# A decoder layer in float32: loaded operands of the Q, K and V products placed 64 bytes ahead of the streaming ones

## The reference

```
q = x Wq (16 heads of 64);  k = x Wk, v = x Wv (8 groups of 64)
x = norm(x + softmax(mask(q k^T / 8)) v Wout + b_out)          # causal self-attention
xn = norm(x) * ln_w + ln_b;  q = xn Wq' / 8 (8 heads of 64)
x = norm(x + cross(q, ctx Wkv', mask) Wout')                   # over 77 context rows, at most 5 allowed ones
x = norm(x + (silu(x Wg) * (x Wu)) Wd)                         # 768 hidden, integer weights / 127
```

## The kernel before, in words

| product (fills) | loaded | streaming | matmuls a batch |
|---|---|---|---|
| Q, K (nQ0, aQ1 to aQ3, nK0, aK1) | wq, wk | xTs | 72 of 256 columns |
| V (aV0, aV1) | xTs | wv | 12 of 512 columns |
| OUT (oOUT0, oOUT1) | Z | wo | 48 of 256 |
| XQ | xwq | NX | 24 of 256 |
| XV | ctxs (77 columns) | xwv | 6 of 512 |
| XOUT | H | xwo | 24 of 256 |
| FFN (gate and up) | wg, wu | NT | 72 of 256 |
| DOWN | H | wd | 36 of 256 |

## Time and profile before

### The profile page before, as it was taken

One profiled execution on the slowest core, in us unless ns is written; L12 is line 12 of the kernel. 1 busy time (PEld: TensorE's weight loads), 2 busy tenths in 40 slices (PEclk: granted clock), 3 DMA queues, 4 the chain that ended last, 5 costly groups with the idle time before them and its releaser, 6 DMA issues.

```text
span 2029.4 us, 50598 instructions
## 1 busy us (share of the span) xinstructions
PE 2000.8 (99%) x18176; PEld 1837.8 (91%) x18176; DVE 1545.9 (76%) x5708; ACT 1324.1 (65%) x3992; POOL 377.6 (19%) x624
## 2 busy tenths in 40 slices
PE   8999999999999999999999999999999999999987
PEld 7899999999999999999999999999999999999886
DVE  6877777777777777777777777777777777777764
ACT  8866666667666666666666666666666666666642
POOL 3112111211211111112121112112121211121121
PEclk9999999999999999999999999999999999999998
DMA  5100000000000000000000000000000000000000
GB/s 164 32 8 22 19 21 12 11 19 19 22 12 19 11 19 22 19 12 22 8 21 19 12 22 8 22 19 22 12 19 11 19 22 19 12 11 19 13 7 11
DMA packets 49606, 41.19 MB, mean 20 GB/s; under 512 B 19536, under 2 KB 47568, under 8 KB 49360
## 3 DMA queue, kind: packets, MB, share of 16 engines
q1 hardware_dynamic: 49360, 37.96, 6.4%
HBM read 29.56 MB, written 8.39 MB: 19 GB/s over the span
## 4 chain that ended last, share of the span: by engine, by line
PE 97%; DVE 1%; ACT 1%; issue 1%; SPq 0%; DMA 0%; POOL 0%; POOLq 0%; DVEq 0%; ACTq 0%
PE gen L442 20%; PE gen L443 19%; PE gen L444 19%; PE s_ps L582 9%; PE z_ps L624 7%; PE gen L530 3%; PE pt_ps L603 3%; PE gen L543 3%; PE gen L539 3%; PE pt_ps L604 3%; PE pt_ps L608 3%; PE z_ps L626 3%; PE gen L510 2%; PE gen L501 1%; PE gen L554 1%
## 5 line engine op out<-in xcount | busy, mean ns | idle before, releaser
L955 ACT ACTIVATE SM<-SM,least 128x128 f32<-128x128 f32 (+1 forms) x1024 | 452.4, 447 | 35.1 <-DVE least L1480 35.0
L885 ACT ACTIVATE PT<-pt_ps 128x512 f32<-128x512 f32 (+1 forms) x512 | 237.8, 486 | 237.6 <-PE pt_ps L604 235.4
L1480 DVE CUSTOM_DVE_ANT_0 SM<-s_ps,causal 128x128 f32<-128x128 f32 (+1 forms) x1024 | 314.6, 352 | 19.6 <-PE s_ps L582 14.7
L1493 DVE TENSOR_SCALAR SM<-SM,total 128x128 f32<-128x128 f32 (+1 forms) x1024 | 282.7, 339 | 9.1
L1859 POOL TENSOR_TENSOR H_lo<-gated,H_hi 128x256 fp32r<-128x256 f32 x192 | 143.2, 752 | 513.0 <-ACT H_hi L885 513.0
L582 PE MATMUL s_ps<-KT,QT 64*128 64x128 f32 (+1 forms) x2048 | 201.5, 335 | 1.4 <-ACT KT L885 0.7
L938 ACT ACTIVATE gated<-gen 128x256 f32<-128x256 f32 x192 | 73.8, 385 | 197.6 <-PE gen L444 197.5
L955 ACT ACTIVATION_READ_ACCUMULATOR SM<-SM,least 128x1 f32 x1024 | 197.0, 192 | 0.0
L1457 DVE SCALAR_TENSOR_TENSOR gated<-gated,gen 128x256 f32<-128x256 f32 x192 | 80.9, 421 | 115.8 <-ACT gated L938 115.4
L624 PE MATMUL z_ps<-PT,Vt 128*64 128x256 f32 x1024 | 168.1, 399 | 0.0
L582 PEld LDWEIGHTS s_ps<-KT,QT 64*128 64x128 f32 x2048 | 147.6, 187 | 21.8 <-issue 6.4
(11 more groups left out here) (185 smaller groups left out, 6504.7 us busy)
## 6 DMA issues: line engine op xcount, KB each, us to landing
xT_in<-in_xT SPq DMA_DIRECT2D x32, 256.0 KB, 2.9
x_in<-in_x SPq DMA_DIRECT2D x32, 256.0 KB, 2.8
out<-rows SPq DMA_DIRECT2D x32, 256.0 KB, 2.2
ctx_in<-in_ctxT SPq DMA_DIRECT2D x32, 77.0 KB, 2.8
mask_in<-in_maskT SPq DMA_DIRECT2D x32, 77.0 KB, 2.6
SX<-in_wq SPq DMA_DIRECT2D x1, 512.0 KB, 6.4
rows<-in_wv SPq DMA_DIRECT2D x1, 512.0 KB, 7.2
xwk<-in_xwkv SPq DMA_DIRECT2D x1, 512.0 KB, 7.9
```

The source lines that it names most:

```text
L885: return act.activation(o, i, ACT.Copy)
L955: ins = act.activation(part, part, ACT.Exp, scale=-1.0, bias=least[:, i % 4, n:n + 1], accum_out=total[:, i % 4, n:n + 1])
L1480: ins = dve.tensor_tensor_reduce(SM[:, i % 4, at:at + keys], s_ps[bank][:, col:col + keys], causal[:, S - keys:S], -SCALE, -3 * NEG, ALU.a ...
L1493: ins = dve.tensor_scalar(part, part, total[:, i % 4, n:n + 1], None, ALU.mult)
```

## The change

The order of allocation is altered and nothing else. Every tensor keeps its size, and every instruction its operands by name.

```diff
@@ -187,21 +187,21 @@
-        wq_s = halves("wq", [P, KD, HE])
-        wk_s = halves("wk", [P, KD, KE])
         xwq_s = halves("xwq", [P, KD, XE])
         wg_s = halves("wg", [P, KD, HID])
         wu_s = halves("wu", [P, KD, HID])
+        xT_s = halves("xTs", [P, KD, S])
+        least = sb("least", [P, 4, 4])
+        wv_s = halves("wv", [P, KD, KE])
         den = sb("den", [P, T, 2, XH])
-        wv_s = halves("wv", [P, KD, KE])
-        xwv_s = halves("xwv", [P, KD, XE])
-        least = sb("least", [P, 4, 4])
+        wq_s = halves("wq", [P, KD, HE])
+        wk_s = halves("wk", [P, KD, KE])
         wo_s = halves("wo", [P, NP, D])
         xwo_s = halves("xwo", [P, XP, D])
         wd_s = halves("wd", [P, KH, D])
-        xT_s = halves("xTs", [P, KD, S])
         NX_s = halves("NX", [P, KD, S])
         NT_s = halves("NT", [P, KD, S])
+        xwv_s = halves("xwv", [P, KD, XE])
         total = sb("total", [P, 4, 4])
```

## The result

The changed kernel takes 2027.39 us, the median of 20 runs (2025.35 to 2030.22), against 2032.01 of the kernel before in 20 runs beside it (2030.08 to 2034.13): ratio 0.9978, with a 95% interval of 0.9972 to 0.9985. It is 4.6 us faster where 13.8 were forecast. The sign is right, the size is a third.

The account below looks back on a forecast made before the run. It took TensorE, busy throughout, as the bound, so matmul spacing sets the time. Q and K's -9.7 and -4.1 handed on made -13.8 us, from 2031.9 to 2018 us; range for all cases 2010 to 2046.

Parts of the forecast that it names:

- That a nanosecond of a matmul goes to the end: TensorE, whole turn: PE is busy 1798.91 of 1800 us, so any matmul gain or loss reaches the end.
- That placement bears on the rhythm: Matmul spacing: three rhythms for equal shapes don't fit the skill's two-port rule, by which no placement could matter.
- Q and K, own term: Query and key products: 113.3 instead of 117.7 ns between starts, -9.7 us; ends -9.7 and +20.5.
- rival A: The forecast itself: Q and K go to the fast rhythm, 2018 us, range 2010 to 2027; chance 0.44.
- Handed on: DOWN's 36 matmuls and 24 behind the last Q group take over Q and K's rhythm: half of -8.2, -4.1 us.
- V, taken at 0: Value product, 384 matmuls at 233 ns: could gain or lose 2.5 us, so no change assumed.
- XV: Product on xwv, 192 matmuls of 77 loaded columns: plus or minus 1.3 us, taken at 0.
- Entries: First weight loads of Q and K groups beside transposes: changed phases decide the rhythm afresh, priced within the other terms.
- the entry phases and not the offsets make the difference: Sign of being wrong: OUT or XOUT change their rhythm though their offsets haven't; no size given.
- Rival B: Nothing changes, if distance modulo 128 bytes is what matters: 2028 to 2036 us, 2032 in the middle; chance 0.22.
- Rival C: Q and K slower, stream catching the load late: 120 ns or more between starts, up to 2054.9 us without V; chance 0.34.

Follow-up runs that it names:

- the two tries at the fastest: Weights and xTs 64 bytes further on, plus DOWN at -64, Vt, PT moved 64: 2022.89 us; changed kernel with DOWN at -64, ident, SM moved -64: 2020.99 us.

## Why the prediction was right in sign and wrong in size

*That a nanosecond of a matmul goes to the end*: right. The turn is 132 ns shorter, 28 of them make 3.7 us, and the span is 3.6 us shorter. PE is still busy throughout.

*That placement bears on the rhythm*: right. Streams of equal shape, with nothing else running, stood at 113.3 to 120.4 ns, and only the loaded operand's start and what ran ahead differed. The Trainium skill, TensorE: Matmul & The Clock Gate, section Step-by-step, says that loading the next tile doesn't steal read bandwidth from the running matmul. Whatever the ports do, these runs show that the pace is not free of the place, and the measurement decides.

*Q and K, own term, -9.7 us*: this is the step that failed, in its sentence "With the relation mirrored I expect the fast one to be the rule". One of the three groups, 24 matmuls of 72, turned fast; K1, Q1, Q2 and Q3 stayed at 117.7. Measured: -88 ns x 28 = -2.5 us. My argument, that a stream which begins below the load runs over it at once, was a story about one matmul, and no run shows how a stream and a load pass each other. What the runs showed in its place: the streams by themselves have the same two rhythms at -64 as at +64 and start fast less often (4 of 16 against 12 of 16), Q0 and K0 at -64 are slow again once other tensors stand elsewhere (+106 ns with weights and xTs 64 bytes further on), and the kernel with everything at -64 is 12 us slower. The objection that I wrote under rival A, that the offset alone doesn't choose, was the right one.

*Handed on, -4.1 us*: wrong, in sign too. DOWN is +19 ns a turn and the products behind Q3 +3, together +0.6 us. The rhythm is handed on, as I read it from the earlier trace rows, and in one kernel even through transposes. But the load that joins the two products decides whether it passes: at 0 it broke, at 64 it gave 166 ns a turn. I had left that load's relation out; the change moved it from 64 to 0.

*V, taken at 0*: measured -52 ns, -1.4 us, inside the ends of plus and minus 2.5. *XV*: +14 ns with what follows it, +0.4 us, inside its 1.3.

*Entries, without a price of their own*: first gate products -25, second half of XQ -38, gate and up behind V +38, together -25 ns or -0.7 us. The prediction had named them as a sign for itself ("the entry phases and not the offsets make the difference"), for OUT and XOUT; they came at XQ and the gate. Moving ident alone has the same effect on the first two, though ident stays put in the changed kernel.

Sum of the measured terms: -2.5 + 0.6 - 1.4 + 0.4 - 0.7 = -3.6 us.

*Rival B*: its condition is refuted; the period is 256 bytes and not 128 (120.0 at 0, 118.7 at 128), yet its picture, most groups as they were, was nearer than mine. The time of 2027.4 lies between my range for A, which ended at 2027, and B's, which began at 2028. *Rival C*: 120 ns or more in Q and K exists at relation 0 and not at -64. The kernel with everything at -64 is slower by the slow rhythm in OUT, XOUT and the gate and up products, and not in the way that C had it. (The shares given under the rivals add up to 0.36 for slower and 0.19 for same, not 0.35 and 0.20.)

What stays open: what sets the entry of a group. Which rhythm Q0 and K0 take behind the value products was predicted wrongly twice, in the two tries at the fastest. The runs show that it depends on the places of other tensors (ident alone turned three stretches) and on the rhythm before; the rule that gives it is not found. No run tells whether more of an address than its place modulo 256 counts for it. Nor was it measured inside the memory why 0, 64 and 192 differ: two reads that disturb each other would fit, but no run sees them.

## What to carry to other kernels

Where TensorE is busy throughout with short matmuls, start addresses modulo 256 bytes were worth up to 6% of a product here (113.3 against 120.0 ns). With 256 streaming columns keep loaded minus streaming off 0, and prefer +64 to -64: its streams started fast more often, and all products at -64 cost 12 us. With 512 columns that order did not hold: V was faster at -64, by 4 ns a matmul. Read it in start-to-start distances in the timeline, not in durations; and look at the load that joins two products as at a third relation. A change of the order of allocation reaches products whose operands keep their relation, so judge such an edit by a table of all stretches of a turn, and expect single groups to turn either way.

## What the hardware showed that I had not expected

- Two stable rhythms for identical instructions on identical addresses, 113.3 and 117.7 ns, kept until something ahead or between disturbs them (16 of 16 pairs within a relation); a slow stream did not heal by itself.
- The rhythm can survive six transposes of 128 columns: in 28 of 28 turns of the kernel with weights and xTs 64 bytes further on, though not in the kernels before and after.
- Of 16 relations stepped by 16 bytes, only 64 and 192 ever reached 113.3 ns with 256 columns.
- Where the one load of 128 columns between two products stands costs or saves 154 to 166 ns over the 36 matmuls behind it.
